# Pass 0 of a linear-attention and ternary-FFN kernel, laid out anew over its 160 products

## What is computed

```python
q = xn @ Wq + bq ; k = xn @ Wk + bk ; v = xn @ Wv + bv     # per head
qf = elu(q) + 1 ; kf = elu(k) + 1
# causal linear attention in chunks of 128 tokens
out = (qf @ state + tril(qf @ kf.T) @ v) / (qf . running_sum(kf) + 1e-6)
s = out @ Wo + bo
xn2 = layernorm(xn) * ln_w + ln_b
scale = mean(abs(W)) ; Wt = clip(round(W / scale), -1, 1)
g = silu(xn2 @ Wt)
y = x + s * g
```

## Time and profile before

| | us |
|---|---|
| median of 3 runs | 2769.86 |
| lowest and highest | 2537.55, 2785.28 |
| the profiled execution | 2535.86 |
| its span on the slowest core (core 2) | 2534.3 |
| spans of all cores | 2526.8 to 2534.3 |
| TensorE busy (PE) | 2410.5 (95%) |
| VectorE busy (DVE) | 1370.7 (54%) |
| ScalarE busy (ACT) | 813.6 (32%) |
| GpSimd busy (POOL), DMA issues | 254.3 (10%) |

### The profile page before, as it was taken

How to read it: one execution, slowest core, us unless ns; L and a number is a source line. 1 busy time by engine, 2 the same in 40 slices (tenths; PEclk the granted TensorE clock), 3 DMA queues, 4 the chain that set the end, 5 groups by cost and what they waited for, 6 DMA issues and landing times.

```text
span 2534.3 us, 39052 instructions; the slowest of 8 cores (2526.8 to 2534.3 us)
## 1 busy us (share of the span) xinstructions
PE 2410.5 (95%) x12749; PEld 1168.0 (46%) x13002; DVE 1370.7 (54%) x2414; ACT 813.6 (32%) x1458; POOL 254.3 (10%) x452
## 2 busy tenths in 40 slices
PE   1798989899999999999999999999999999999998
PEld 0344444444444455554444455554444445554443
DVE  2414887765542367765553167766454247766443
ACT  0134556531210255551110055553110035554000
POOL 1000000011210000001111000001111000000110
PEclk9899999999999999999999999999999999999999
DMA  9896555458885533238896543326888553322651
GB/s 192 204 249 145 122 153 175 117 148 209 210 197 92 103 60 64 68 94 203 209 205 127 94 94 59 77 52 156 235 187 185 96 94 67 68 63 64 169 159 71
DMA packets 158500, 338.20 MB, mean 133 GB/s; under 512 B 78432, under 2 KB 78432, under 8 KB 150112
## 3 DMA queue, kind: packets, MB, share of 16 engines
q0 software_dynamic: 56320, 201.36, 38.7%
q1 hardware_dynamic: 101120, 134.24, 18.8%
q10 hardware_dynamic: 864, 0.10, 0.0%
HBM read 411.14 MB, written 41.94 MB: 179 GB/s over the span
## 4 chain that ended last, share of the span: by engine, by line
PE 87%; DMA 5%; DVE 2%; issue 2%; ACT 2%; SPq 1%; DVEq 0%; ACTq 0%; POOL 0%; POOLq 0%
PE pj L836 48%; PE pj L850 32%; DMA stg<-w_f 4%; SPq L265 1%; DMA xln<-x 1%; PE po L900 1%; PE px L864 1%; PE po L903 1%; PE px L890 1%; PE pa L871 1%; PE px L880 1%; PE pj L930 1%; ACT stg L498 1%; DVE bst L574 0%; DVE tern L706 0%
## 5 line engine op out<-in xcount | busy, mean ns | idle before, releaser
L836 PE MATMUL pj<-ring,big 128*128 128x512 bf16 x6017 | 1331.2, 381 | 76.1 <-DMA big<-xn 68.6
L836 PEld LDWEIGHTS pj<-ring,big 128*128 128x128 bf16 x6144 | 601.8, 98 | 796.4 <-issue 83.6
L850 PE MATMUL pj<-big,ring 128*128 128x512 bf16 x3970 | 905.1, 380 | 17.8 <-ACT er L460 10.8
L850 PEld LDWEIGHTS pj<-big,ring 128*128 128x128 bf16 x4096 | 391.8, 98 | 447.0 <-issue 22.4
L458 ACT ACTIVATE ee<-pj,bq 128x512 f32<-128x512 f32 x128 | 87.8, 686 | 540.7 <-PE pj L850 538.9
L594 DVE TENSOR_TENSOR big<-pj,brow 128x512 bf16<-128x512 f32 x128 | 87.8, 689 | 314.1 <-PE pj L836 294.7
L721 DVE SCALAR_TENSOR_TENSOR tf<-pj,r,c_b 128x512 f32<-128x512 f32 x128 | 95.4, 749 | 236.3 <-PE pj L836 225.5
L554 ACT ACTIVATE sg<-tf 128x512 bf16<-128x512 f32 x128 | 79.7, 629 | 328.3 <-DVE tf L721 328.1
L393 POOL DMA_DIRECT2D ring<-w_qk x128 | 69.0, 557 | 946.7 <-PE pj L850 639.3
L635 DVE TENSOR_TENSOR_SCAN cum<-kh,kc 128x512 f32<-128x512 bf16 x128 | 163.2, 1275 | 0.0
L458 ACT ACTIVATE ee<-pj,bk 128x512 f32<-128x512 f32 x128 | 87.8, 686 | 207.3 <-PE pj L850 207.3
(11 more groups left out here) (67 smaller groups left out, 1591.0 us busy)
## 6 DMA issues: line engine op xcount, KB each, us to landing
ring<-w_qk POOLq DMA_DIRECT2D x128, 512.0 KB, 11.3
xln<-x SPq DMA_DIRECT2D x32, 1024.0 KB, 7.5
ring<-w_v POOLq DMA_DIRECT2D x64, 512.0 KB, 14.7
stg<-w_f SPq DMA_DIRECT2D x32, 1024.0 KB, 7.3
ring<-wscf POOLq DMA_DIRECT2D x64, 512.0 KB, 8.2
ring<-w_o POOLq DMA_DIRECT2D x64, 512.0 KB, 10.7
xy<-x SPq DMA_DIRECT2D x128, 256.0 KB, 4.5
y<-xy POOLq DMA_DIRECT2D x128, 256.0 KB, 4.9
```

Source lines behind the costliest of these rows:

```text
L836: last = tensor.matmul(bank[:, :], src(k, m), ring[c % 3][:, k * 512:(k + 1) * 512], start=(k == 0), stop=(k == NT - 1))
L850: last = tensor.matmul(bank[:, :], ring[c % 3][:, base + k * 256:base + k * 256 + 128], x[:, k * T + tok:k * T + tok + 512], start=(k == 0 ...
```

## The change

- **Start.** SP loads x tiles 0 to 3 into four buffers (`xfirst`: the two `xln` and two of `stg`), 4 to 7 as tiles are normalised. GpSimd loads chunk 0 after x tile 0 is there, chunk 1 after three tiles are normalised, chunk 2 after six products. In pass 0 an x tile is transposed by 16 TensorE transposes into `px`, `pa` and `po`, one tile ahead of its product, and ScalarE copies it to `big`.
- **Pieces of w_f.** `stg` has three buffers. ScalarE's sums stand at products 17, 19, ... 29 and at slots 1, 3, ... 17; the scale is at slot 20.
- **Ternary weight.** Half a piece (1024 columns) after every second slot, 23 to 85, on VectorE; weighed by ScalarE one slot later; two `tern` buffers, three `wpr` (over `stg`).
- **Constant row.** GpSimd multiplies each 512 columns of ternary weight with its column of ln_b and adds them up in `c_b`, 64 times; TensorE sums over the partitions and broadcasts with one product of fp32 ones (128 rows).
- **LayerNorm of the next pass.** One tile at products 122, 126, ... 150 in pass 0 and 104, 110, ... 146 in passes 1 and 2, on all engines.
- SP's and GpSimd's queues are written product by product; the biases come as 128 rows instead of one row read 128 times.

```diff
-SCALE_SLOT = 15
-def tern_slot(b):
-    return 17 + (11 * b) // 4
+SCALE_SLOT = 20
+def tern_slot(hb):
+    return 23 + 2 * hb
+TERN_AT = {tern_slot(hb): hb for hb in range(32)}
+B_AT = {tern_slot(8 * n + 7) + 5: n for n in range(4)}
+def abs_step(a):
+    return 17 + 2 * a if a < 7 else QK0 + 2 * (a - 7) + 1
+def ln_step(p, m):
+    return 122 + 4 * m if p == 0 else 104 + 6 * m
...
         def _(sync):
+            def load_first(m):
+                if m >= 4:
+                    sync.wait_ge(s_xn, m - 3)
+                sync.dma_start(out=xfirst[m % 4][:, :],
+                               in_=x_in[m * 128:(m + 1) * 128, :]
+                               ).then_inc(s_x[m % 4], 16)
...
+            def load_piece(k):
+                n, q = divmod(k % 16, 4)
+                if k < 3:
+                    sync.wait_ge(s_xn, MT)
+                elif k < 19:
+                    sync.wait_ge(s_abs, k - 2)
+                else:
+                    b = k - 19
+                    sync.wait_ge(s_wst[(b + 16) % 3], 16 * (b // 3 + 1))
...
-            load_x(0)
-            load_x(1)
-            load_bias(0, 0)
-            load_bias(0, 1)
-            for m in range(MT):
-                transpose_x(m)
-                if m + 2 < MT:
-                    load_x(m + 2)
+            load_first(0)
+            load_first(1)
+            load_bias(0, 0)
+            load_first(2)
+            load_first(3)
+            load_bias(0, 1)
+            for m in range(4, MT):
+                load_first(m)
...
         def _(gpsimd):
+            def constants(k):
+                n, i = divmod(k, 16)
+                b = k // 4
+                acc = c_b[:, n * 512:(n + 1) * 512]
+                piece = tern[b % 2][:, (k % 4) * 512:(k % 4 + 1) * 512]
+                gpsimd.wait_ge(s_ter, k // 2 + 1)
+                if i == 0:
+                    gpsimd.tensor_scalar(acc, piece, lnb[:, 0:1], None, ALU.mult
+                                         ).then_inc(s_acc, 1)
+                else:
+                    gpsimd.wait_ge(s_acc, k)
+                    chained(gpsimd.tensor_scalar(part[:, :], piece, lnb[:, i:i + 1],
+                                                 None, ALU.mult))
+                    gpsimd.tensor_tensor(acc, acc, part[:, :], ALU.add
+                                         ).then_inc(s_acc, 1)
+            gpsimd.wait_ge(s_x[0], 16)
+            load_chunk(0)
+            gpsimd.wait_ge(s_xn, 3)
+            load_chunk(1)
+            gpsimd.wait_ge(s_mm, 6)
+            load_chunk(2)
+            for p in range(NP):
+                for i in range(NG):
+                    if p == 0 and i - 1 - QK0 in TERN_AT:
+                        constants(2 * TERN_AT[i - 1 - QK0])
+                    if p == 0 and i - 2 - QK0 in TERN_AT:
+                        constants(2 * TERN_AT[i - 2 - QK0] + 1)
+                    c = p * NCHUNK + (i + 1) // 8 + 2
+                    if i % 8 == 7 and c < NP * NCHUNK:
+                        load_chunk(c)
...
         def _(scalar):
+            def copy_x(m):
+                for half in range(2):
+                    scalar.wait_ge(s_tr, 2 * m + half + 1)
+                    last = scalar.copy(
+                        xbuf(0)[:, :].rearrange("p (i t) -> p i t", t=T)[
+                            :, half * 8:half * 8 + 8, m * 128:(m + 1) * 128],
+                        blocks(ptr[(2 * m + half) % 4][:, :]))
+                last.then_inc(s_xc, 1)
...
+            ln_rs(0)
+            ln_rs(1)
             for m in range(MT):
-                ln_rs(m)
-            for a in range(16):
-                abs_piece(a)
+                copy_x(m)
+                if m + 2 < MT:
+                    ln_rs(m + 2)
...
         def _(vector):
-            def ternary(b):
+            def ternary(hb):
+                b = hb // 2
                 k = 16 + b
+                c0 = (hb % 2) * 1024
+                t = tern[b % 2][:, c0:c0 + 1024]
+                w = stg[k % 3][:, c0:c0 + 1024]
...
+                if b >= 2:
+                    vector.wait_ge(s_acc, 2 * hb - 6)
+                    vector.wait_ge(s_wp, hb - 3)
+                chained(vector.tensor_scalar(t, w, thr[:, 1:2], None, ALU.is_lt))
+                vector.scalar_tensor_tensor(t, w, thr[:, 0:1], t, ALU.is_gt,
+                                            ALU.subtract).then_inc(s_ter, 1)
...
+            ln_stats(0)
+            ln_apply(0)
+            ln_stats(1)
+            ln_apply(1)
+            ln_stats(2)
             for p in range(NP):
+                for i in range(NG):
+                    if p == 0 and i + 3 < MT:
+                        ln_stats(i + 3)
+                    if p == 0 and i + 2 < MT:
+                        ln_apply(i + 2)
+                    if i < QK0:
+                        evict_v(p, i // 8, i % 8)
...
         def _(tensor):
-                if t in C_AT:
...
                 if t in B_AT:
                     n = B_AT[t]
                     bank = take_bank(("b", n))
-                    tensor.wait_ge(s_c3, n + 1)
-                    tensor.matmul(bank[:, :], ones_f[0:3, :], c3[0:3, :],
+                    tensor.wait_ge(s_acc, 16 * n + 16)
+                    tensor.matmul(bank[:, :], ones_f[:, :],
+                                  c_b[:, n * 512:(n + 1) * 512],
                                   start=True, stop=True).then_inc(s_bmm, 1)
+            def transpose_x(m):
+                tensor.wait_ge(s_xn, m + 1)
+                if m >= 2:
+                    tensor.wait_ge(s_xc, m - 1)
+                for half in range(2):
+                    bank = ptr[(2 * m + half) % 4]
+                    for k in range(8):
+                        c0 = (half * 8 + k) * 128
+                        last = tensor.transpose(bank[:, k * 128:(k + 1) * 128],
+                                                xn[m % 2][:, c0:c0 + 128],
+                                                identb[:, :])
+                    last.then_inc(s_tr, 1)
...
+                    if i < MT:
+                        if p == 0:
+                            if i + 1 < MT:
+                                transpose_x(i + 1)
+                            tensor.wait_ge(s_xc, i + 1)
```

More of the change, by code:

```diff
@@ L33, with stores_by, of_fo @@
 LAST_SLOT = 68
-SCALE_SLOT = 15
-def tern_slot(b):
-    return 17 + (11 * b) // 4
[L42 to L48, removed]
+SCALE_SLOT = 20
[5 more added lines that the diff above has]
+    return 17 + 2 * a if a < 7 else QK0 + 2 * (a - 7) + 1
+ABS_AT = {abs_step(a): a for a in range(16)}
+def ln_step(p, m):
+    return 122 + 4 * m if p == 0 else 104 + 6 * m
+LN_AT = [{ln_step(p, m): (p + 1) * MT + m for m in range(MT)} if p + 1 < NP else {}
+         for p in range(NP)]
+def stores_by(b, j):
+    return (b - j + 2) // 3
+def of_fo(i):
+    n, m = divmod(i - FO0, 16)
+    return n, m % 8, m >= 8
 def turn_of_banks():
@@ L263, in transpose_x @@
                 p, m = divmod(g, MT)
+                if g == MT:
+                    for j in range(3):
+                        sync.wait_ge(s_wst[(j + 16) % 3], 16 * stores_by(16, j))
+                    sync.wait_ge(s_acc, 64)
+                if m == 0 and p > 1:
+                    sync.wait_ge(s_mm, (p - 1) * NG)
                 sync.wait_ge(s_xn, g + 1)
@@ new lines, in _ @@
+                for i in range(NG):
+                    if p == 0:
+                        ternary(i)
+                    if i in (8, 16, 24, 32):
+                        load_bias(p, i // 8 + 1)
+                    if i < FO0:
+                        continue
+                    n, m, o = of_fo(i)
+                    if not o and m < 4:
+                        load_xr(p, n, m)
+                    if o and 2 <= m < 6:
+                        load_xr(p, n, m + 2)
+                    if i + 5 in LN_AT[p]:
+                        load_x(LN_AT[p][i + 5])
+                    if i - 2 in LN_AT[p]:
+                        transpose_x(LN_AT[p][i - 2])
+                    if o and m == 7:
+                        if n < 2:
+                            load_bias(p, 6 + n)
+                        elif p + 1 < NP:
+                            load_bias(p + 1, n - 2)
@@ L387, in load_chunk @@
                     if p == 0:
-                        gpsimd.wait_ge(s_wst[0], 16 * (2 * n + 2))
-                        gpsimd.wait_ge(s_wst[1], 16 * (2 * n + 2))
+                        for j in range(3):
+                            gpsimd.wait_ge(s_wst[(j + 16) % 3],
+                                           16 * stores_by(4 * n + 4, j))
                 else:
@@ L404, in store_y @@
                     in_=xy[k % 4][:, :]).then_inc(s_ys[k % 4], 16)
[L406 to L417 removed]
+            chain = 0
```

357 lines of the change are left out of this document (146 added, 211 removed).

## The result

The changed kernel took 2520.02 us (median of 20 runs), the kernel before 2542.03 us over as many: a ratio of 0.9865, with a 95% interval of 0.9835 to 0.9895. It took 2518.64 us (span 2517.0) instead of 2535.86: 17 us gained of 74 forecast. By the ratio the gain is some 34 us. The forecast was 2462 us, range 2438 to 2500.

What follows compares the result with a forecast made beforehand. TensorE, busy 99% in later passes, was the bound; only pass 0's surplus of 144.6 us could be won. Start 34.6 plus 55.9 in the rest, less 17, gives 73.5 us: 2535.86 to 2462 us, range 2438 to 2500.

Steps and rivals of the forecast that it cites:

- LayerNorm spread: Passes 0 to 2: LayerNorm moves between F and O products, where TensorE has no wait; 0 taken, at most 24 us.
- Start: Pass 0's first eight products: the eighth ends at 72.5 instead of 107.1 us, 34.6 us saved (bounds 22 and 44).
- ScalarE's wait of 10.8 us: Pass 0: TensorE's wait for ScalarE's eviction goes once w_f pieces are spread over V stage and odd slots; 10.8 us.
- the low clock priced at 10.5 us: Pass 0: the granted clock of 0.98 over 525.5 us goes with the `prod` waits, worth 10.5 us.
- VectorE and GpSimd: Q/K slots of pass 0: GpSimd delays VectorE 1.0 us per attention unit (two slots); 17 us lost waiting at `prod`.
- the meeting that was priced: GpSimd beside VectorE's first ternary instruction, likened to a DMA issue taking 1.56 instead of 0.55 us; 1.0 us a unit.
- rival B: Exclusive engines: GpSimd holds VectorE except beside PSUM readers, middle 2.4 us a unit; 45 us, 2490 us; chance 0.18.
- Rival A: GpSimd costs VectorE nothing: no 17 us lost, 2445 us; chance 0.24.
- C: Old waits change names: w_f pieces late (10.8 us), VectorE bunches keep `prod` late with its clock (30); 2486 us; chance 0.10.
- rival D: GpSimd's chain of 64 constants becomes the bound, deciding from 3.9 us each; 2612 us at 6.5 us; chance 0.04.
- one of the signs that I had named for being wrong: The prediction counts as wrong if TensorE waits on GpSimd's sums for the constant row.
- Passes 1 to 3: Second and third pass stay at 595.4 us each, since the change takes no TensorE work out of them.

## Why the prediction failed, step by step

The step that failed is "LayerNorm spread": "I take 0", at most 24 us. I priced VectorE's and ScalarE's part of it and not its DMA. The row for it stood in my own text: the transposing DMA that was held for 29.21 us beside the weight quarters. I read it as a property of the start. The runs show that it comes back later: some 600 us after the start, beside weights, x loads and stores, a transposition was held for up to 31.8 us. The kernel before kept its later ones apart: on core 2, the eight in pass 0 began 16.6 to 31.8 us after the last weights were issued, with no x load just ahead, and took 1.3 to 4.0 us. In the changed kernel they stand four products apart, and on core 7 two of them began 7.2 and 13.2 us after the weights and took 10.6 and 31.8. Core 7 lost 41.2 us by it in waits, and its last stage of pass 0 is 45.8 us longer than core 4's. With a plain copy in its place, or with TensorE transposing five products behind the LayerNorm, no core of the profiled execution is above 2486 us. Since the metric is the slowest of eight cores, one long meeting on any of them is paid: in the ten runs the fastest core took 2468 to 2477 us, and the slowest was above 2500 in eight.

Not all of that is the transposing DMA. The lower granted clock of cores 2 and 3 would have kept the profiled execution at 2505 us without any wait on core 7, and two of the eight runs above 2500 carry that mark on their slowest cores. The prediction has no such term either: it took the granted clock of the undisturbed stages for all cores.

The rest, on core 4:

- **Start.** Forecast: first product ends at 41, eighth at 72.5. Its evictions show 40.3 and 73.2; core 7 has 43.8 and 76.5. Right, by its steps: 28.42 us for the last of the first weights, and 4.9 us a tile (L684 begins at 40.32, 45.33, 50.28 and 54.89).
- **V stage.** 24 products at 3.455 us: 82.9 us. Right.
- **ScalarE's wait of 10.8 us.** Gone. Right. So is the low clock priced at 10.5 us: core 4 has 1.00 in both stretches, with 13.8 us of waits for `prod` left.
- **VectorE and GpSimd.** Forecast: 1.0 us a unit, 17 us of waits for `prod`, none over 2. Measured: 0.605 + 0.516 us more in the two L699 of a unit and 0.07 in `prod`, 1.2 us; 13.8 us of waits, 17 of at most 0.9 us. The size is right, by luck, for the meeting that was priced did not take place. It was one of GpSimd with the first ternary instruction, of the one-input kind. That one (L799) took 740 to 746 ns in all 20, and the second (L800) 1283 to 1286; GpSimd's sums wait for L800, and none of them ran beside either. What grew is L699, which reads two fp32 tiles from SBUF. That is the kind of meeting of rival B, at half of B's 2.4 us a unit. Rival A (nothing) falls, B in its size (45 us), and C.
- **GpSimd's own price.** I bounded an instruction by 0.69 and 1.27 us. The add took 1.41 us and the multiply 1.68 in the mean: too low. A pair is near 3.2 us, short of the 3.9 from which rival D decides, but a broadcast waited 3.9 us for the sums: a small term that I had at nothing, and one of the signs that I had named for being wrong.
- **Passes 1 to 3.** From the eviction of the fourth V product of pass 1 to the end core 4 needs 2471.2 - 690.96 = 1780.2 us, the kernel before 2534.3 - 753.90 = 1780.4. Right.
- **Small slips in the working.** What is left of 65.1 us is 5.0, not 4.2; 9.05 - 8.24 is 0.81 us a unit, not 0.85. Neither moves the forecast by more than 1 us.

So core 4's pass 0 is 676.9 us against 740.0 - 73.5 = 666.5 forecast. Most of the 10 us is waits behind the V stage: 24 us (13.8 for `prod`, 5.0 at the F and O evictions, 3.9 for the broadcast, 1.6 others) against 17. The sum was right to 10 us for the best core, which has no long meeting and no low clock; it was forecast as if all eight were such.

On the Trainium skill, SBUF — State Buffer, "Who interferes with whom": the rule that two-input VectorE instructions meet GpSimd's reads is borne out for the one with two fp32 inputs (681 to 1286 ns), and for `prod` only now and then (0.95 us beside a GpSimd add at 261.67 on core 4, 1.6 us once, and 684 ns in the median with an add beside nearly every one). For the running sum, which reads one bf16 tile twice, it is hardly borne out: 1283 ns in the mean beside GpSimd's sums and 1274 without them, and once, beside a multiply at 257.67, 1.45 us.

## What to carry to other kernels

A DMA transposition had no price of its own here: 1.3 to 5.1 us where the kernel before placed it after its start, and up to 32.7 us among weight loads, x loads and stores. When a change moves one, list what each queue has in flight at its new place, and give it the duration of the worst row, not of the median one. With a metric of the slowest of eight cores, a stall on any one core is the price; TensorE transposes for 0.9 to 1.05 us a tile, asked for once the tile is surely ready, were the cheaper way in the crowded pass. Read the spans and the granted clock of all cores before giving one cause to their spread: here the slow cores had two.

## What was not expected of the hardware, and what stays open

- Beside a long transposing DMA the stores of another queue are late too: issued within 0.14 us of each other, the two took 31.8 and 32.6 us. The DMA engines were busy and moved 59 GB/s. Beside the plain copy of the same bytes it was 267, and no store took over 20.2 us.
- Two neighbouring cores had a granted clock of 0.81 for some 160 us, with TensorE busy throughout, while core 4 had 1.00. Why is open.
- GpSimd multiplies 512 bf16 columns by a scalar in 1.59 us (median), longer than it adds two fp32 tiles of 512 (1.27 us).
- What in a meeting does it is open: how much of a meeting is due to the weight quarters and how much to the x tile's own load, which the new spacing also brings next to each transposition, wasn't tried apart. The two runs that only moved the places (ratios 0.978 and 0.989) don't separate them. Distance from the weights alone does not decide: on core 7 a transposition 21.3 us after them took 13.77 us, and on core 4 one some 9 us after them 12.45. Whether the stores are late because of the transposition or of what delays it too isn't shown either, except that the plain copy ends both.
